# GQA and cross attention joined: the last GQA pair also does the first rows, queries and scores of the cross layer, and the cross layer's pairs run in another order

## The chip, the cores and the metric

The kernel runs on one core of one Trainium2 chip. The metric is the device time of one execution in microseconds (us), the median of the runs. A core has five engines that run side by side, each in its own program order, and meet only at semaphores: TensorE (PE in the profile, PEld its weight loads), VectorE (DVE), ScalarE (ACT), GpSimd (POOL), and SyncE (SP), which issues the DMA transfers here. TensorE's clock has two levels, 1.2 and 2.4 GHz; the profile gives the granted clock as a share of the higher.

## The reference, cut to what matters

Four layers follow one another on `x` (16 rows of 128 positions by 512) with the context `ctx_2048` of the same shape.

```python
x = _L0_xattn_ref(ctx_2048, x, ...)   # latent attention, RMS norm, MLP
x = _L1_xattn_ref(x, ctx_2048, ...)   # grouped attention (GQA): LN(attention(x, ctx) Wo + bo + x) gamma + beta
x = _L2_xattn_ref(x, ctx_2048, ...)   # cross attention, MLP
x = _L3_xattn_ref(ctx_2048, x, ...)   # latent attention, RMS norm, MLP

# _L2_xattn_ref (cross), shortened
x = layer_norm(hidden_states, ln1_w, ln1_b)
q = x @ q_w + q_b
k = encoder_hidden_states @ k_w + k_b
v = encoder_hidden_states @ v_w + v_b
attn = softmax(where(mask, q k^T / sqrt(HD), mask_value))     # 16 heads of 32
hidden = (attn v) @ cproj_w + cproj_b + hidden_states
y = layer_norm(hidden, ln2_w, ln2_b)
return hidden + gelu(y @ fc_w + fc_b) @ proj_w + proj_b
```

Each row depends only on itself: row b of the cross layer needs row b of GQA alone.

## The kernel before, in words

The 16 rows go through a layer in 8 pairs. Each layer has one function per engine (`pe_gqa`, `act_gqa`, `dve_gqa`, `pool_gqa`, `sp_gqa` and the same with `cross`), which lists that engine's work by hand. The order in these lists is the order of execution.

A pair has rounds: four in GQA, two in cross. A round is: scores on PE into four score banks (`pe_scores`; in cross a mask matmul closes each bank), a maximum on DVE (`dve_max`), exponentials on ACT with the row sum (`act_exp`, four segments for each of four banks; in cross they read the score bank and free it, in GQA DVE has copied the scores already), the reciprocal on DVE (`dve_invert`), the multiplication on POOL (`pool_norm`, 16 instructions), the transposes of the probabilities on PE (`pe_turn_probs`, four times four), their copies out of PSUM (two on ACT, `act_probs`; two on DVE, `dve_probs`), and the product with the values (`pe_attend`). Then the heads are taken out with a high and a low part (`act_heads`, `dve_heads`), the output projection runs for each row (`pe_out`), DVE adds the residual and takes the moments (`dve_out`), and POOL normalizes (`pool_root`). In GQA the normalized row is the cross layer's residual; it is normalized once more for the cross layer's queries (`dve_again`, `pool_again`), and SP stores both to HBM.

All products are float32 in three passes over high and low parts (`three_passes`, L324). Inputs of a pair are loaded, turned by PE (`pe_turn_x`), taken out by ACT and DVE (`act_x`, `dve_x`) and projected (`pe_queries`). In cross `act_x` is eight small activations with the layer norm's scale and bias into the buffer `affine` (L780), and `dve_x` makes the high part (L1064) and the low part (L1066) from it. Cross keys and values are computed during GQA, stored to HBM and reloaded per pair.

All PSUM results but the scores go through a ring of four banks (`begin`): each waits until the result four before it has been taken out. `act_round` and `dve_round` interleave one round's maxima or exponentials with the copies of another's transposes, and call `between()`, which holds the `act_x` or `dve_x` of a next pair. In the cross layer before, `between()` is filled in round 1 of a pair, for the next pair.

In a cross pair PE's list is: scores of round 1, transposes of round 0, x transposes of the next pair, output of the odd row of the last pair, attend 0, queries of the next pair (two blocks), scores of round 0 of the next pair, transposes of round 1, output of the even row, attend 1. Between the layers PE does the last GQA output (row 15), the x transposes, queries and first scores of cross pair 0. On DVE the order there is: `dve_again` of row 14, `dve_out` of row 15, `dve_again` of row 15, mask, `dve_x` of cross pair 0, and POOL does the normalizations of rows 14 and 15 between, then two tile splits (`split_tile`) of the cross output weights.

## Time and profile before

| | us |
|---|---|
| timed runs, median (lowest, highest) | 2624.87 (2624.17, 2631.24) |
| the profiled execution | 2633.31 |
| its span in the trace | 2631.4 |
| PE busy | 2473.8 (94%) |
| ACT, POOL, DVE busy | 1088.4, 1114.7, 1224.5 |
| mean granted clock of TensorE | 0.971 |

PE is busy in nearly all of the span. What is not PE time, or is PE time at the lower clock, shows in the slices of the page and in stretches of the trace. The GQA layer lies at about 840 to 1212 us from the span's start, the cross layer's attention at about 1212 to 1482, its MLP behind. All times of stretches and rows below are in us from the span's start.

### The profile page before, as it was taken

Reading aid. Unit: us, or ns where it says so; the run is one execution under the profiler, and the core shown is the slowest. Engines: PE = TensorE matmul, PEld = TensorE weight load, DVE = VectorE, ACT = ScalarE, POOL = GpSimd, SP = SyncE. Lnnn points to the kernel's source line nnn. Section 1 sums busy time; section 2 is a strip of 40 time slices with the busy share of each in tenths; the row PEclk is TensorE's granted clock in tenths of the full one; section 3 lists DMA queues with packets and bytes.
Section 4 is the critical chain, followed back from the end, with each engine's and each line's share of the span. In section 5 each row is a group of like instructions: output and inputs, shape, how many; then the busy total and the mean of one; then the engine's idle time right before and its main releaser. Section 6 shows DMA issues by size and latency. Waiting matters only on the chain.

```text
span 2631.4 us, 48760 instructions
## 1 busy us (share of the span) xinstructions
PE 2473.8 (94%) x18464; PEld 2073.3 (79%) x18464; DVE 1224.5 (47%) x3295; ACT 1088.4 (41%) x3705; POOL 1114.7 (42%) x1972
## 2 busy tenths in 40 slices
PE   7999998999999999986888899999999999899999
PEld 5888886888888888875777788887788888688887
DVE  4555555233224677674555532332355555432322
ACT  4555554111115777774666311111455555311111
POOL 2453445500063778776575740014144443730000
PEclk9999999999999999996898999999999999999999
DMA  4111312211033232223343330122112211320100
GB/s 158 58 57 57 102 53 81 76 48 49 28 95 107 96 122 99 88 82 126 109 142 121 123 97 18 48 68 65 49 50 79 68 41 57 101 66 31 49 32 16
DMA packets 106614, 198.07 MB, mean 75 GB/s; under 512 B 8272, under 2 KB 35600, under 8 KB 103312
## 3 DMA queue, kind: packets, MB, share of 16 engines
q1 hardware_dynamic: 106384, 194.97, 22.4%
q8 instruction: 149, 2.44, 0.4%
q14 instruction: 81, 0.66, 0.1%
HBM read 136.22 MB, written 58.72 MB: 74 GB/s over the span
## 4 chain that ended last, share of the span: by engine, by line
PE 77%; ACT 10%; DVE 7%; POOL 3%; issue 2%; DMA 1%; SPq 0%; DVEq 0%; POOLq 0%; ACTq 0%
PE banks L324 69%; ACT plain_high L715 7%; PE banks L465 4%; PE banks L495 3%; DVE plain_high L970 1%; POOL plain_high L1298 1%; ACT plain_high L699 1%; ACT plain_work L780 1%; DVE stats L1101 1%; PE banks L519 1%; DVE rounded_work L1075 1%; DVE rounded_high L1019 1%; DMA rounded_work<-ctx_split 0%; POOL rounded_high L315 0%; DVE plain_work L1116 0%
## 5 line engine op out<-in xcount | busy, mean ns | idle before, releaser
L324 PE MATMUL banks<-rounded_work,rounded_low 128*128 128x512 f32 (+1 forms) x2688 | 526.0, 350 | 45.2 <-DVE rounded_low L1130 13.7
L1298 POOL TENSOR_SCALAR plain_high<-plain_high,inv_sum 128x128 f32<-128x128 f32 (+1 forms) x1024 | 389.4, 405 | 416.3 <-DVE inv_sum L992 415.9
L324 PEld LDWEIGHTS banks<-rounded_work,rounded_low 128*128 128x128 f32 x2688 | 435.6, 193 | 114.1 <-issue 29.2
L324 PE MATMUL banks<-rounded_work,rounded_high 128*128 128x512 f32 (+1 forms) x2400 | 487.6, 357 | 7.4 <-DMA rounded_work<-ctx_split 7.1
L949 ACT ACTIVATE plain_work<-banks,columns 128x512 f32<-128x512 f32 x192 | 132.5, 690 | 866.9 <-PE banks L324 866.9
L324 PEld LDWEIGHTS banks<-rounded_work,rounded_high 128*128 128x128 f32 x2400 | 398.1, 192 | 75.7 <-DMA rounded_work<-ctx_split 7.7
L1274 DVE CAST rounded_work<-plain_work 128x512 fp32r<-128x512 f32 x192 | 102.1, 532 | 694.0 <-ACT plain_work L949 685.8
L324 PE MATMUL banks<-rounded_low,rounded_work 128*128 128x512 f32 x1728 | 418.2, 394 | 0.0
L324 PE MATMUL banks<-rounded_high,rounded_work 128*128 128x512 f32 (+1 forms) x1728 | 390.2, 377 | 0.0
L324 PEld LDWEIGHTS banks<-rounded_low,rounded_work 128*128 128x128 f32 x1728 | 324.6, 190 | 69.9 <-issue 3.3
L324 PEld LDWEIGHTS banks<-rounded_high,rounded_work 128*128 128x128 f32 x1728 | 309.1, 188 | 60.6 <-issue 1.4
L1442 POOL TENSOR_TENSOR plain_work<-plain_work 128x512 f32<-128x512 f32 x48 | 66.7, 1420 | 613.1 <-DMA plain_work<-x 417.6
L974 DVE TENSOR_REDUCE neg_max<-banks 128x2 f32<-128x512 f32 (+1 forms) x320 | 204.7, 682 | 36.0 <-PE banks L454 36.0
L1298 POOL TENSOR_SCALAR plain_low<-plain_low,inv_sum 128x256 f32<-128x256 f32 x256 | 118.8, 488 | 235.4 <-DVE inv_sum L992 235.4
L715 ACT ACTIVATE plain_high<-banks,neg_max 128x256 f32<-128x256 f32 (+1 forms) x512 | 210.1, 464 | 12.3 <-DVE neg_max L974 12.3
L715 ACT ACTIVATE plain_high<-plain_high,neg_max 128x128 f32<-128x128 f32 x512 | 197.8, 391 | 17.5 <-DVE neg_max L970 17.5
L465 PE MATMUL banks<-ident,plain_high 128*128 128x128 f32 x1280 | 181.1, 297 | 13.4 <-POOL plain_high L1298 9.1
L465 PEld LDWEIGHTS banks<-ident,plain_high 128*128 128x128 f32 x1280 | 154.0, 152 | 33.6 <-issue 18.4
L1276 DVE TENSOR_TENSOR rounded_work<-plain_work,rounded_work 128x512 fp32r<-128x512 f32 x192 | 155.8, 811 | 6.6
L324 PE MATMUL banks<-rounded_work 32*128 32x256 f32 (+1 forms) x3072 | 132.4, 299 | 27.0 <-DVE rounded_work L1046 20.3
L324 PEld LDWEIGHTS banks<-rounded_work 32*128 32x128 f32 x3072 | 109.6, 194 | 60.7 <-issue 55.4
L992 DVE RECIPROCAL inv_sum<-row_sum 128x4 f32<-128x4 f32 (+1 forms) x224 | 41.6, 186 | 211.7 <-ACT plain_high L715 168.7
(101 smaller groups left out, 3069.8 us busy)
## 6 DMA issues: line engine op xcount, KB each, us to landing
plain_work<-x SPq DMA_DIRECT2D x96, 256.0 KB, 3.2
plain_work<-mlp_w SPq DMA_DIRECT2D x96, 256.0 KB, 2.7
rounded_work<-ctx_split SPq DMA_DIRECT2D x16, 1024.0 KB, 6.0
u<-plain_work SPq DMA_DIRECT2D x48, 256.0 KB, 2.6
plain_work<-u SPq DMA_DIRECT2D x12, 1024.0 KB, 7.2
x<-plain_work SPq DMA_DIRECT2D x48, 256.0 KB, 2.2
plain_work<-attention_w SPq DMA_DIRECT2D x44, 256.0 KB, 2.7
plain_work<-inputs_t SPq DMA_DIRECT2D x8, 1024.0 KB, 8.0
```

What stands on the lines that cost most here:

```text
L324: mm = pe.matmul(dst, lhs(i), rhs(j), start=first and n == 0, stop=last and n == 2, skip_group_check=True)
L465: mm = pe.transpose(dst[:, t * P:(t + 1) * P], pr[:, r, t * P:(t + 1) * P], ident[:, :])
L495: mm = pe.matmul(dst[32 * r:32 * r + 32, i * P:(i + 1) * P], v, pt[:, r, at:at + P], start=t == 0, stop=t == n_t - 1, skip_group_check=True)
L519: mm = pe.transpose(dst[:, r * P:(r + 1) * P], u_nat[:, r, f * P:(f + 1) * P], ident[:, :])
L715: last = act.activation(pr[:, r, part], pr[:, r, part] if gqa else PS[:, r, part], ACT.Exp, scale=-1.0 if gqa else 1.0, bias=neg_max[:, R ...
L949: act.activation(gelu[:, j % 2, :], bank(key), ACT.Gelu_apprx_tanh, bias=col(y, 28 + j)).then_inc(evac_of(key), 1)
L974: dve.tensor_reduce(neg_max[:, R % 2, r, 0:y.segs], src.rearrange("p (g n) -> p g n", g=y.segs), AX.X, ALU.max, negate=True).then_inc(maxe ...
L992: dve.reciprocal(inv_sum[:, R % 2, 2 * half:2 * half + 2, 0:y.segs], row_sum[:, R % 2, 2 * half:2 * half + 2, 0:y.segs]).then_inc(inverted, 1)
L1274: dve.tensor_copy(G[:, j % 4, 0, :], gelu[:, j % 2, :]).then_inc(g_hi, 1)
L1276: dve.tensor_tensor(G[:, j % 4, 1, :], gelu[:, j % 2, :], G[:, j % 4, 0, :].bitcast(F32), ALU.subtract).then_inc(g_ready, 1)
L1298: last = pool.tensor_scalar(part, part, inv_sum[:, R % 2, r, g:g + 1], 1.0, ALU.mult, ALU.mult)
L1442: last = pool.tensor_tensor(res[:, r, :], res[:, r, :], wide_bias, ALU.add)
```

## The change

The joint and the cross layer's own order are rewritten on all five engines. Line numbers of the changed kernel differ by a few; the instructions are the same, but for their order and the buffers they use.

In the last GQA pair, where the next pair's inputs and queries would stand, now stand those of cross pair 0, its first scores, and the x transposes of cross pair 1. The GQA output of row 15, its moments and normalizations move into cross pair 0. In the cross pairs the queries of the next pair move up behind the transposes of round 0; attend 0 and the odd row's output stand behind them; the x transposes are those of two pairs ahead and stand behind the transposes of round 1, with `between()` now in the round 0 of the next pair.

```diff
@@ pe_gqa (last pair)
-                if more:
-                    pe_turn_x(pe, y, p + 1)
+                pe_turn_x(pe, *((y, p + 1) if more else (L[2], 0)))
...
-                if more:
-                    pe_queries(pe, y, p + 1, 0)
+                pe_queries(pe, *((y, p + 1) if more else (L[2], 0)), 0)
...
                 if more:
                     pe_values(pe, y, p + 1, 0)
+                else:
+                    pe_queries(pe, L[2], 0, 1)
                 pe_attend(pe, y, p, 2)
                 if more:
                     pe_values(pe, L[2], p + 1, 0)
                     pe_scores(pe, y, p + 1, 0)
+                else:
+                    pe_scores(pe, L[2], 0, 0)
                 pe_turn_probs(pe, y, p, 3)
+                if not more:
+                    pe_turn_x(pe, L[2], 1)
...
-            pe_out(pe, y, B - 1)
@@ pe_cross
-            pe_turn_x(pe, y, 0)
-            for i in range(2):
-                pe_queries(pe, y, 0, i)
-            pe_scores(pe, y, 0, 0)
             for p in range(PAIRS):
                 more = p + 1 < PAIRS
                 pe_scores(pe, y, p, 1)
                 pe_turn_probs(pe, y, p, 0)
-                if more:
-                    pe_turn_x(pe, y, p + 1)
-                if p:
-                    pe_out(pe, y, 2 * p - 1)
-                pe_attend(pe, y, p, 0)
                 if more:
                     for i in range(2):
                         pe_queries(pe, y, p + 1, i)
                 else:
                     for f in range(FB):
                         pe_turn_u(pe, M[y.n], 0, f)
+                pe_attend(pe, y, p, 0)
+                pe_out(pe, *((y, 2 * p - 1) if p else (L[1], B - 1)))
                 if more:
                     pe_scores(pe, y, p + 1, 0)
                 pe_turn_probs(pe, y, p, 1)
+                if p + 2 < PAIRS:
+                    pe_turn_x(pe, y, p + 2)
                 pe_out(pe, y, 2 * p)
                 pe_attend(pe, y, p, 1)
@@ dve_cross
-                dve_round(dve, y, p, 1, (p, 0), inputs)
-                if p:
-                    dve_out(dve, y, 2 * p - 1)
-                dve_heads(dve, y, p, 0)
+                dve_round(dve, y, p, 1, (p, 0), nothing)
...
-                dve_round(dve, y, p + 1, 0 if more else None, (p, 1), nothing)
+                dve_heads(dve, y, p, 0)
+                if p:
+                    dve_out(dve, y, 2 * p - 1)
+                else:
+                    dve_again(dve, L[1], B - 2)
+                    dve_out(dve, L[1], B - 1)
+                dve_round(dve, y, p + 1, 0 if more else None, (p, 1), inputs)
+                if not p:
+                    dve_again(dve, L[1], B - 1)
                 dve_out(dve, y, 2 * p)
                 dve_heads(dve, y, p, 1)
@@ pool_gqa (last pair)
+                if not more:
+                    pool.wait_ge(k_stored, 16 * PAIRS)
+                    pool.wait_ge(v_stored, 16 * PAIRS)
+                    split_tile(pool, ("qo", 2), 4)
+                    split_tile(pool, ("qo", 2), 5)
                 pool_norm(pool, y, p, 3)
                 pool_bias(pool, y, 2 * p + 1)
-                if more:
-                    pool_norm(pool, y, p + 1, 0)
+                if not more:
+                    split_tile(pool, ("qo", 2), 6)
+                pool_norm(pool, *((y, p + 1) if more else (L[2], 0)), 0)
                 pool_root(pool, y, 2 * p)
-            pool_again(pool, y, B - 2)
-            pool_root(pool, y, B - 1)
-            pool_again(pool, y, B - 1)
@@ pool_cross
                 pool_norm(pool, y, p, 1)
+                if not p:
+                    split_tile(pool, ("qo", 2), 7)
+                    pool_again(pool, L[1], B - 2)
+                    pool_root(pool, L[1], B - 1)
                 pool_bias(pool, y, 2 * p)
...
                 if more:
                     pool_norm(pool, y, p + 1, 0)
+                if not p:
+                    pool_again(pool, L[1], B - 1)
                 pool_bias(pool, y, 2 * p + 1)
```

ACT's lists change in the same way as DVE's. SP loads the first cross rows, keys and output weight tiles during the last GQA pair, and the first rows of the MLP (`sp_first_rows`) one pair earlier. So that the first cross round can begin while GQA's probabilities are in use, the cross layer's probabilities and heads move from the slots 12 to 15 to the slots 0 to 3 (`plain_low` and `rounded_low` in the rows below), with the MLP's weight blocks in another order of slots, one buffer of the cross keys moves, and the affine rows of cross pairs 0 and 1 get a buffer of their own (`first_affine`).

PE, at the joint, before. The names: L495 is the attend (`plain_work` in GQA, `plain_high,plain_work` in cross), L324 with `rounded_high` alone an output projection, L359 the x transposes, L324 with 128x256 the queries, L324 with 128x128 and L454 the cross scores with their mask, L465 the transposes of probabilities.

```order
L324 MATMUL banks<-rounded_high 128x512 x12
L495 MATMUL banks<-plain_work 32x128 x16
L324 MATMUL banks<-rounded_high 128x512 x12
L359 MATMUL banks<-ident,plain_work 128x128 x8
L324 MATMUL banks<-rounded_work,rounded_low 128x256 x48
L324 MATMUL banks<-rounded_work 128x128 x48
L454 MATMUL banks<-plain_work,ones_row 128x512 x4
L324 MATMUL banks<-rounded_work 128x128 x48
L454 MATMUL banks<-plain_work,ones_row 128x512 x4
L465 MATMUL banks<-ident,plain_high 128x128 x16
```

The same place on PE after the change, from the attend of GQA's round 2.

```order
L495 MATMUL banks<-plain_work 32x128 x16
L324 MATMUL banks<-rounded_work 128x128 x48
L454 MATMUL banks<-plain_work,ones_row 128x512 x4
L465 MATMUL banks<-ident,plain_high 128x128 x16
L359 MATMUL banks<-ident,plain_work 128x128 x8
L324 MATMUL banks<-rounded_high 128x512 x12
L495 MATMUL banks<-plain_work 32x128 x16
L324 MATMUL banks<-rounded_work 128x128 x48
L454 MATMUL banks<-plain_work,ones_row 128x512 x4
L465 MATMUL banks<-ident,plain_low 128x128 x16
L324 MATMUL banks<-rounded_work,rounded_low 128x256 x48
```

The first cross scores now stand before GQA's last transposes, and the queries of pair 0 stand still further up, one block in each of two GQA rounds.

PE, one cross pair before, from the scores of round 1.

```order
L324 MATMUL banks<-rounded_work 128x128 x48
L454 MATMUL banks<-plain_work,ones_row 128x512 x4
L465 MATMUL banks<-ident,plain_high 128x128 x16
L359 MATMUL banks<-ident,plain_work 128x128 x8
L324 MATMUL banks<-rounded_low,rounded_high 128x512 x12
L495 MATMUL banks<-plain_high,plain_work 32x128 x16
L324 MATMUL banks<-rounded_work,rounded_low 128x256 x48
L324 MATMUL banks<-rounded_work 128x128 x48
L454 MATMUL banks<-plain_work,ones_row 128x512 x4
L465 MATMUL banks<-ident,plain_high 128x128 x16
L324 MATMUL banks<-rounded_low,rounded_high 128x512 x12
L495 MATMUL banks<-plain_high,plain_work 32x128 x16
```

The same pair after the change.

```order
L324 MATMUL banks<-rounded_work 128x128 x48
L454 MATMUL banks<-plain_work,ones_row 128x512 x4
L465 MATMUL banks<-ident,plain_low 128x128 x16
L324 MATMUL banks<-rounded_work,rounded_low 128x256 x48
L495 MATMUL banks<-plain_low,plain_work 32x128 x16
L324 MATMUL banks<-rounded_low 128x512 x12
L324 MATMUL banks<-rounded_work 128x128 x48
L454 MATMUL banks<-plain_work,ones_row 128x512 x4
L465 MATMUL banks<-ident,plain_low 128x128 x16
L359 MATMUL banks<-ident,plain_work 128x128 x8
L324 MATMUL banks<-rounded_low 128x512 x12
L495 MATMUL banks<-plain_low,plain_work 32x128 x16
```

The queries (128x256) moved from directly before the next scores to directly behind the first transposes, and the x transposes (L359) from the first half of the pair to the second.

ACT, one cross pair before, from the copies and exponentials in which round 0 is transposed. L699 is a copy of transposed probabilities, L715 the exponentials, L780 the affines, L729 the heads, L755 the queries.

```order
L699 ACTIVATE plain_high<-banks 128x512
L715 ACTIVATE plain_high,row_sum<-banks,neg_max 128x128 x4
L699 ACTIVATE plain_high<-banks 128x512
L715 ACTIVATE plain_high,row_sum<-banks,neg_max 128x128 x4
L780 ACTIVATE plain_work<-banks,columns 128x128 x8
L715 ACTIVATE plain_high,row_sum<-banks,neg_max 128x128 x8
L729 ACTIVATE rounded_high<-banks,columns 128x128 x4
L755 ACTIVATE rounded_work<-banks,columns 128x256 x4
L699 ACTIVATE plain_high<-banks 128x512
```

ACT after, from the same place.

```order
L697 ACTIVATE plain_low<-banks 128x512
L713 ACTIVATE plain_low,row_sum<-banks,neg_max 128x128 x4
L697 ACTIVATE plain_low<-banks 128x512
L713 ACTIVATE plain_low,row_sum<-banks,neg_max 128x128 x12
L753 ACTIVATE rounded_work<-banks,columns 128x256 x4
L727 ACTIVATE rounded_low<-banks,columns 128x128 x4
L697 ACTIVATE plain_low<-banks 128x512
L713 ACTIVATE plain_low,row_sum<-banks,neg_max 128x128 x4
L697 ACTIVATE plain_low<-banks 128x512
L713 ACTIVATE plain_low,row_sum<-banks,neg_max 128x128 x4
L778 ACTIVATE plain_work<-banks,columns 128x128 x8
L713 ACTIVATE plain_low,row_sum<-banks,neg_max 128x128 x8
```

The affines (L780, now L778) moved from the exponentials of round 1 to those of the next pair's round 0, and the queries stand before the heads.

## Rows read from the trace of the kernel before

**Rows 1.** Stretches: from:to, length, busy PE PEld DVE ACT POOL, granted clock, DMA share, GB/s.
```profile
1168.96:1276.06 107.10, 72.60 (x729) 61.64 (x729) 50.68 (x197) 55.21 (x244) 66.30 (x134) 0.75 0.29 105
1276.06:1453.55 177.49, 151.29 (x1682) 129.81 (x1681) 105.69 (x259) 120.24 (x528) 115.25 (x257) 0.91 0.39 133
1453.55:1482.19 28.64, 20.44 (x150) 15.92 (x149) 19.85 (x43) 14.12 (x49) 21.39 (x37) 0.88 0.29 93
```

**Rows 2.** Timeline of PE at the joint: start, duration, instructions, [idle before <-releaser].
```profile
1209.50 2.99 PE L324 MATMUL banks<-rounded_high 128*128 128x512 f32 x12 [1.53 <-issue]
...
1224.49 8.10 PE L324 MATMUL banks<-rounded_work,rounded_low 128*128 128x256 f32 x48 [11.13 <-issue]
1234.63 1.58 PE L324 MATMUL banks<-rounded_work 32*128 32x128 f32 x48 [2.04 <-DVE rounded_work L1046]
```

**Rows 3.** Timeline of DVE at the joint.
```profile
1220.90 0.69 DVE L1101 BATCH_NORM_STATS2 stats<-plain_work 128x6 f32<-128x512 f32 x1 [4.51 <-POOL plain_work L1333]
...
1222.18 0.42 DVE L1064 CAST rounded_work<-plain_work 128x512 fp32r<-128x512 f32 x1
```

**Rows 4.** Timeline of PE in one cross pair.
```profile
1315.30 6.00 PE L324 MATMUL banks<-rounded_work,rounded_low 128*128 128x256 f32 x48 [1.30 <-DVE rounded_work L1066]
1323.34 1.59 PE L324 MATMUL banks<-rounded_work 32*128 32x128 f32 x48 [2.04 <-DVE rounded_work L1046]
...
1325.25 3.42 PE L465 MATMUL banks<-ident,plain_high 128*128 128x128 f32 x16
1328.43 3.02 PE L324 MATMUL banks<-rounded_low,rounded_high 128*128 128x512 f32 x12
1331.38 1.08 PE L495 MATMUL banks<-plain_high,plain_work 128*32 128x128 f32 x32
...
1334.85 2.22 PE L465 MATMUL banks<-ident,plain_high 128*128 128x128 f32 x16
...
1344.27 1.21 PE L324 MATMUL banks<-rounded_work,rounded_low 128*128 128x256 f32 x8 [1.28 <-DVE rounded_work L1066]
```

**Rows 5.** Chain of waits in the same pair: start, duration, engine and line.
```profile
1321.33 0.85 ACT rounded_work L755 x2
1322.21 0.89 DVE rounded_work L1046 x2
...
1326.40 0.60 ACT plain_high L699
1327.00 1.40 ACT plain_high L715 x8
1328.40 0.49 ACT plain_high L699
...
1340.23 2.81 ACT plain_work L780 x8
...
1343.52 0.70 DVE rounded_work L1066
```

**Rows 6.** Timeline of ACT: the heads right behind GQA's last exponentials.
```profile
1198.50 0.60 ACT L729 ACTIVATE rounded_high<-banks,columns 128x128 fp32r<-128x128 f32 x2
```

**Rows 7.** Groups by form, 1276 to 1453.6: count, busy us, mean ns, idle before.
```profile
L1298 POOL TENSOR_SCALAR plain_high<-plain_high,inv_sum 128x128 f32<-128x128 f32 x194 | 68.4, 379 | 58.2 <-DVE inv_sum L992 58.2
```

**Rows 8.** Stretches in the cross layer, columns as in rows 1.
```profile
1305.92:1309.68 3.76, 3.19 (x28) 2.56 (x24) 3.73 (x12) 2.42 (x10) 3.68 (x8) 1.00 0.30 117
1325.00:1329.00 4.00, 4.00 (x23) 3.66 (x20) 3.03 (x5) 2.60 (x12) 0.94 (x2) 0.59 0.37 135
1352.30:1359.00 6.70, 6.68 (x69) 6.26 (x69) 2.72 (x5) 2.29 (x10) 2.43 (x4) 0.50 0.31 108
```

**Rows 9.** Timeline of PE in the tail of the cross layer.
```profile
1470.23 0.66 PE L465 MATMUL banks<-ident,plain_high 128*128 128x128 f32 x4 [1.58 <-ACT plain_work L800]
...
1477.74 4.61 PE L324 MATMUL banks<-rounded_low,rounded_high 128*128 128x512 f32 x12 [2.42 <-DVE rounded_high L1019]
```

More of the change, by code:

```diff
@@ L938, in act_cross @@
                         act_turn_u(act, M[y.n], 0, f)
-                act_round(act, y, p + 1, 0 if more else None, (p, 1), nothing)
+                act_heads(act, y, p, 0)
+                act_round(act, y, p + 1, 0 if more else None, (p, 1), inputs)
                 act_heads(act, y, p, 1)
@@ L1619, in sp_gqa @@
                     sp_next_hidden(sp, y, 2 * p)
+                if not more:
+                    load_tile(sp, ("qo", 2), 6)
+                if p:
                     sp_store_h(sp, y, 2 * p - 1)
```

142 lines of the change are left out of this document (62 added, 80 removed).

## The prediction

> **What bounds the kernel now.** I read the stretches by engine first [rows 1]. All columns are of the one core; times are us from the span's start. In the 107.1 us from the scores of the last GQA pair to the first full cross pair, PE is busy 72.6 us at a granted clock of 0.75 of full speed. In the six cross pairs behind it PE is busy 151.3 of 177.5 us at 0.91, in the tail of 28.6 us 20.4 us. Everywhere else the page shows PE at nine tenths or more, so only these three stretches, here A, B and C, can give much.
>
> Then the PE timeline of the joint [rows 2]: the last output rows of GQA, 11.13 us of idle time, the queries of cross pair 0, and more idle time around its first scores. The profile calls the 11.13 us "issue"; the DVE rows tell what it is [rows 3]. DVE stood 4.51 us for POOL's normalization (L1333) of row 15 and only then, at 1222.18, could split the turned rows of cross pair 0 that PE needs. That is a chain of orders, not of data: the rows of pair 0 have nothing to do with row 15.
>
> Then a cross pair on PE [rows 4]: 1315.30 to 1344.27 is one pair. Its idle times are 2.04 us before the scores (the query split on DVE), 1.28 to 1.30 us before the queries (the split of the x rows), and small ones. Over six pairs the period is 177.49/6 = 29.6 us [rows 1]. The chain of waits of that pair [rows 5] is mostly ACT: copies, exponentials, the affine of the x rows.
>
> **The change, stretch A.** In the last GQA pair ACT gets cross affines (eight activations, 2.81 us, [rows 5]) where it had no inputs; that delays its later rounds by 2.8 us. The first query block adds 0.85 us on ACT and 0.89 us on DVE [rows 5], about 1 us of it on the path. ACT reached the end of the last GQA exponentials at 1198.50 [rows 6]; now 1198.5 + 2.8 + 1.0 = 1202.3. Behind it come the second query block, 0.85 + 0.89 + 0.25 of hand-over, so the first cross scores start at 1204.3. (Before: 1234.63 [rows 2].) POOL's two tile splits ahead of the last GQA norm end that norm near 1208.3, off this path, since the x transposes behind it are wanted by ACT only at 1210.7.
> From there, at full clock:
> - scores 1.9 ([rows 4], 1323.34 to 1325.25), first transposed block and its hand-over 0.6: 1206.8;
> - ACT, copy 0.60, exponentials 1.40, copy 0.49, exponentials 1.40, affines 2.81 = 6.7 [rows 5]: 1213.5;
> - DVE's split of the last x block 0.1 + 0.44 + 0.70 (the second is [rows 5]) = 1.2, the reciprocal and hand-over 0.4, sixteen POOL multiplies at 68.4/194 us each = 5.65 [rows 7], the last transposes 0.6: 1221.4;
> - queries 6.0, attend 1.0, output rows 2.95 [rows 4]: 1231.3; scores 1.9, first block 0.6: 1233.8;
> - ACT 6.7 + the other two exponentials 2.8 = 9.5, hand-over 0.1, scores 1.8: 1245.2.
> Before, this point (the end of the scores of round 1 of cross pair 1) is 1276.06 [rows 1]. The gain is 30.9 us at full clock. It is not all kept. The present stretch runs at 0.75; the new one still idles on PE (3.6 us ahead of the first scores, 2 to 3 us twice later). A fall there costs PE half of the 4.0 to 6.7 us that one lasts [rows 8], 2 to 3.4 us, and part of it is under POOL's time. I take 4 us for two or three falls (bounds 1 and 8). POOL and SP are late in pair 1: the deferred norm of row 15, its store, and the reload of the buffer put POOL's second bias at about 1254, and the norm of round 1 of pair 1 ends 0.7 us after PE wants it. So A gives 30.9 - 4 - 0.7 = 26 (22 to 29).
> What hides the moved work: the GQA output of row 15 (2.95 us on PE) now stands between pair 1's queries and scores, in time in which PE would wait; its normalization (DVE stood 4.51 us for it, [rows 3]) fits POOL's gaps, which was busy 66.3 of the 107.1 us. If that cover is gone, its 4.5 us come back, once.
>
> **Stretch B.** The new pair order puts the queries right behind the transposes of round 0; attend and an output (4 us) now stand between the queries and the scores, which covers the 2.04 us. The x rows are turned one pair early, so the 1.3 us goes too. What is late next: the affines now sit in round 0 of ACT, between its second and third exponentials, and round 1's scores on PE need the last exponential to free its bank. The loop from scores to scores is, in the same terms as above, 0.6 + 6.7 + 1.2 + 0.4 + 5.65 + 0.6 (the norm path) + queries 6.0 + 1.0 + 2.95 + scores 1.9 = 27.0 us. The other branch, through the freed bank, is 0.6 + 9.5 + 0.1 + 1.9 + 2.0 (transposes) + 6.0 + 1.0 + 2.95 + 1.9 = 25.95, so PE has 1.05 us of slack there. PE's own work is about 22.7 us (6.0 + two scores 3.7 + two transposes 4.0 + x transposes 1.1 + two outputs 5.9 + two attends 2.0): it will stand some 2.8 us before round 1's scores and 1.1 us inside the transposes behind them. The two small waits are thus replaced by one larger one. The pair shown took 28.97 with 1.2 us lost to the clock in one transpose group (the sixteen transposes of 1325.25 took 3.42 us, those of 1334.85 2.22, [rows 4]), so the old period at full clock is 27.8 and the average loss 1.8.
> The new wait will make the clock fall too, I think: both falls of [rows 8] followed idle times of 2.0 and 1.3 us within some 9 us. One fall costs 2 to 3.4 us; 1.05 of it is under POOL's time. I take 1.1 net: 28.1 us, or 1.5 less than 29.6. Six periods: 9 us (bounds 27.0, a gain of 15.6, and 29.6, nothing).
>
> **Stretch C.** The transposes for the MLP move ahead of the attend, and ACT's and DVE's part ahead of the heads. Stepping through with the same durations I get out-to-end 24.7 us from the end of the last scores instead of 28.6 [rows 1, 9], with a new PE wait of 3.2 us before the attend, for the first MLP block's evacuation; less 2 us for the clock: 2 us (0 to 4). The reload of the MLP rows one pair early and the other block order of the MLP move no time: PE is busy without a gap there.
>
> **Sum.** 26 + 9 + 2 = 37 us. The profiled execution has a span of 2631.4 and 2633.31 us; it would become 2594.4 and 2596.3. The three timed runs lie lower, median 2624.87; the same 37 us off that is 2588.
>
> **A page against the rows.** The row first: from 1305.92 to 1309.68 PE does 3.76 us of almost nothing but transposes, with 0.55 us of waiting, and the granted clock stays at 1.00, the 2.4 GHz level [rows 8]. The Trainium skill, TensorE: Matmul & The Clock Gate, Part 4: PE-mode transpose, states that transposes do not count as PE busy in the way matmuls do. By that rule the new order, a wait of 2.8 us, 1.9 us of scores and then transposes with gaps, is what the gate punishes, and the time is that of the last rival below; by the row it is my forecast.
>
> **The rivals.** (1) B's period does not shrink: the larger wait costs a fall of 6.7 us in each pair, [rows 8] at 1352.3, or ACT's chain is longer than I added. For it: ACT is the largest part of the chain. 26 + 0 + 2 = 28: 2597. Chance 0.20. (2) The clock never falls in B and the loop runs at 27.0: 28 + 15.6 + 3 = 46.6: 2578. For it: after the wait of 1.30 us the 48 query matmuls still ran at full speed, 6.00 us, and so they do in all six pairs. Chance 0.17. (3) The join does not join: pair 1's residual rows wait for the deferred row 15 (POOL norm, store, reload of the one buffer), SP's queue holds the x rows and keys behind it, and A gives 10 us less: 2598. Against it: I find 4 us of slack at the bias. Chance 0.08. (4) Slower: the low clock (1.2 GHz) begins at round 1's scores in every pair and lasts through the queries. Then scores 1.9, transposes 2.0 and queries 6.0 double, less the 1.05: 27.0 + 8.85 = 35.9, six times 6.3 more than now, +38, against the 28 of A and C: 2635. It decides from a period of 29.6 + 28/6 = 34.3. Against it: no fall in B lasted more than 7 us, and the transposes of [rows 8]. Chance 0.04.
>
> **How the numbers follow.** Forecast 0.50, rivals 0.20, 0.17, 0.08, 0.04, and 0.01 for the rest. The forecast alone spans 2580 to 2597; with rivals 1 and 2 and most of 3 the range is 2574 to 2604. A measurement of this kernel can tell 0.3%, 7.9 us, from no change. All cases but rival 4 and part of 3 are faster by more: faster 0.94, same 0.02, slower 0.04.
>
> **What would show it.** In the profile after: no PE idle of over 4 us between the last GQA pair and cross pair 1; the end of cross pair 1's second scores near 1249 (1245 at full clock); in the cross pairs a wait of 2 to 3 us before round 1's scores, released by ACT's exponentials, and gaps released by POOL's multiply in the transposes behind; no wait before queries or round 0's scores; a period of 27 to 29 us with one fall of the clock in it. A period over 29.6, or a DVE or POOL wait on the residual rows in pair 1, would prove me wrong.

## The result

The changed kernel takes 2580.59 us (median of 4 runs, 2572.21 to 2583.19) where the kernel before takes 2628.05 on the same chip (2624.17 to 2631.62): a ratio of 0.9827, 95% interval 0.9806 to 0.9848. Two repeats on other chips gave 0.9834 (0.9815 to 0.9852) and 0.9837 (0.9823 to 0.9852). The profiled execution has a span of 2581.3 us where it had 2631.4, so 50.1 us less.

The three stretches of [rows 1] in the profile after, in the same columns: from:to, length, busy PE, PEld, DVE, ACT, POOL, granted clock, DMA share, GB/s. The fourth row is a piece of B with the clock at its lower level, and is discussed further down.

```profile
1167.69:1246.78 79.09, 66.27 (x738) 56.40 (x737) 52.92 (x204) 57.45 (x252) 63.89 (x133) 0.87 0.33 111
1246.78:1407.38 160.60, 146.92 (x1673) 126.84 (x1672) 104.28 (x254) 117.08 (x520) 116.72 (x259) 0.94 0.46 157
1407.38:1433.96 26.58, 20.80 (x150) 17.19 (x149) 16.32 (x42) 14.35 (x49) 19.73 (x33) 0.82 0.32 110
1379.80:1386.30 6.50, 6.49 (x59) 6.06 (x60) 5.39 (x15) 3.12 (x14) 6.22 (x16) 0.50 0.11 47
```

A fell from 107.10 to 79.09 us, B from 177.49 to 160.60, C from 28.64 to 26.58: 28.0 + 16.9 + 2.1 = 47.0 us. The other 3 us lie outside: 1.3 ahead of A and 1.9 behind C. The matmuls are the same; in A the idle time went from 34.5 to 12.8 us, and the granted clock rose from 0.75 to 0.87.

PE at the joint, which answers [rows 2]: start, duration, instructions, [idle before <-releaser].

```profile
1203.08 1.59 PE L324 MATMUL banks<-rounded_work 32*128 32x128 f32 x48 [1.85 <-DVE rounded_work L1044]
...
1208.96 3.01 PE L324 MATMUL banks<-rounded_high 128*128 128x512 f32 x12
...
1220.97 6.70 PE L324 MATMUL banks<-rounded_work,rounded_low 128*128 128x256 f32 x48
...
1228.62 3.06 PE L324 MATMUL banks<-rounded_high 128*128 128x512 f32 x12
```

The first cross scores start at 1203.08, 31.6 us earlier than the 1234.63 of [rows 2], before the last two GQA outputs (1208.96 and 1228.62). The 11.13 us of idle time ahead of the queries of cross pair 0 are gone; from here to the end of A no wait is longer than the 1.85 us shown.

PE in a cross pair, which answers [rows 4]. The rows show the waits ahead of and in one period (from 1300.72, the end of round 1's scores, to the next such end at 1327.81, 27.09 us), and below them the transposes and queries of the period that begins at 1355.00.

```profile
1297.61 0.55 PE L324 MATMUL banks<-rounded_work 32*128 32x128 f32 x3 [1.02 <-ACT plain_low L713]
1299.01 1.33 PE L324 MATMUL banks<-rounded_work 32*128 32x128 f32 x37 [0.85 <-ACT plain_low L713]
...
1300.72 3.63 PE L465 MATMUL banks<-ident,plain_low 128*128 128x128 f32 x16
1304.01 6.21 PE L324 MATMUL banks<-rounded_work,rounded_low 128*128 128x256 f32 x48
1310.14 1.08 PE L495 MATMUL banks<-plain_low,plain_work 128*32 128x128 f32 x32
...
1319.20 3.01 PE L324 MATMUL banks<-rounded_low 128*128 128x512 f32 x12 [0.48 <-ACT plain_low L697]
...
1326.10 1.33 PE L324 MATMUL banks<-rounded_work 32*128 32x128 f32 x37 [0.85 <-ACT plain_low L713]
...
1355.00 1.79 PE L465 MATMUL banks<-ident,plain_low 128*128 128x128 f32 x12
1357.55 0.63 PE L465 MATMUL banks<-ident,plain_low 128*128 128x128 f32 x4 [0.76 <-POOL plain_low L1298]
1357.93 5.99 PE L324 MATMUL banks<-rounded_work,rounded_low 128*128 128x256 f32 x48
1363.85 1.08 PE L495 MATMUL banks<-plain_low,plain_work 128*32 128x128 f32 x32
```

No wait stands before the queries (it was 1.30 us) nor before round 0's scores (it was 2.04). In their place two waits, 1.02 and 0.85 us, stand inside round 1's scores, released by ACT's exponentials. The transposes behind them come in two kinds: at 1300.72 at the low clock and without a gap, 3.29 us until the queries, and at 1355.00 at full clock with a gap that POOL's multiply releases, 2.93 us until the queries.

From these rows a period at full clock throughout can be put together, though no period of this trace is one. The transposes take 2.93 us (1355.00 to 1357.93), the queries 5.92 (1357.93 to 1363.85), and from the attend to the end of round 1's scores it is 17.67 (1310.14 to 1327.81). The sum is 26.52 us. The 17.67 us come out the same in the first four periods.

The chain of waits in such a pair, which answers [rows 5]:

```profile
1289.48 0.60 ACT plain_low L697
1290.08 1.00 ACT plain_low L713 x6
...
1293.37 2.79 ACT plain_work L778 x8
1296.16 2.81 ACT plain_low L713 x16
1298.97 0.04 issue
1299.01 1.33 PE banks L324 x37
```

ACT's affines (2.79 us) now lie on the chain between the exponentials. The tail, which answers [rows 9], has the predicted wait of 3.2 us before the attend and keeps the 2.4 us before its last output:

```profile
1416.07 1.08 PE L495 MATMUL banks<-plain_low,plain_work 128*32 128x128 f32 x32 [3.25 <-ACT plain_work L798]
...
1429.62 4.54 PE L324 MATMUL banks<-rounded_low 128*128 128x512 f32 x12 [2.43 <-DVE rounded_low L1017]
```

### The profile page after: what moved, and what is told of

Its sections match the earlier page's. It is cut to its first block, busy times and chain, and to the rows that moved or that the text cites. A ratio compares the mean times of both kernels' runs of the same rounds, so it can differ in the third digit from the quotient of the medians.

```text
span 2581.3 us, 48757 instructions
## 1 busy us (share of the span) xinstructions
PE 2461.0 (95%) x18464; PEld 2065.3 (80%) x18464; DVE 1227.5 (48%) x3295; ACT 1087.8 (42%) x3705; POOL 1110.2 (43%) x1972
## 3 DMA queue, kind: packets, MB, share of 16 engines
q1 hardware_dynamic: 106384, 194.97, 22.6%
## 4 chain that ended last, share of the span: by engine, by line
PE 81%; ACT 9%; DVE 6%; POOL 2%; DMA 1%; issue 1%; SPq 0%; DVEq 0%; POOLq 0%; ACTq 0%
PE banks L324 71%; PE banks L465 5%; ACT plain_high L713 4%; PE banks L495 3%; ACT plain_low L713 2%; DVE plain_high L968 2%; ACT plain_work L778 1%; DVE stats L1099 1%; PE banks L519 1%; POOL plain_low L1298 1%; DVE rounded_work L1073 1%; DMA rounded_work<-ctx_split 1%; DVE plain_work L977 1%; PE banks L454 0%; ACT plain_work L697 0%
## 5 line engine op out<-in xcount | busy, mean ns | idle before, releaser
L324 PE MATMUL banks<-rounded_work,rounded_low 128*128 128x512 f32 (+1 forms) x2688 | 528.1, 351 | 23.2 <-DVE rounded_low L1128 13.8
L324 PEld LDWEIGHTS banks<-rounded_work,rounded_low 128*128 128x128 f32 x2688 | 438.0, 194 | 90.0 <-issue 18.0
L324 PE MATMUL banks<-rounded_work,rounded_high 128*128 128x512 f32 (+1 forms) x2400 | 485.8, 356 | 9.3 <-DMA rounded_work<-ctx_split 8.9
L324 PEld LDWEIGHTS banks<-rounded_work,rounded_high 128*128 128x128 f32 x2400 | 397.0, 191 | 77.0 <-DMA rounded_work<-ctx_split 9.6
L1298 POOL TENSOR_SCALAR plain_high<-plain_high,inv_sum 128x128 f32<-128x128 f32 (+1 forms) x768 | 296.0, 408 | 335.1 <-DVE inv_sum L990 334.7
L324 PE MATMUL banks<-rounded_low,rounded_work 128*128 128x512 f32 x1728 | 416.3, 392 | 0.0
L324 PE MATMUL banks<-rounded_high,rounded_work 128*128 128x512 f32 (+1 forms) x1728 | 390.2, 377 | 0.0
L324 PEld LDWEIGHTS banks<-rounded_low,rounded_work 128*128 128x128 f32 x1728 | 323.2, 189 | 69.1 <-issue 3.0
L324 PEld LDWEIGHTS banks<-rounded_high,rounded_work 128*128 128x128 f32 x1728 | 309.1, 188 | 60.6 <-issue 1.4
L1298 POOL TENSOR_SCALAR plain_low<-plain_low,inv_sum 128x128 f32<-128x128 f32 (+1 forms) x512 | 209.2, 430 | 272.9 <-DVE inv_sum L990 272.5
L713 ACT ACTIVATE plain_low<-banks,neg_max 128x128 f32<-128x128 f32 (+1 forms) x512 | 210.3, 465 | 5.2 <-DVE neg_max L972 5.1
L324 PEld LDWEIGHTS banks<-rounded_work 32*128 32x128 f32 x3072 | 109.6, 190 | 56.7 <-issue 39.7
L324 PE MATMUL banks<-rounded_work 32*128 32x256 f32 (+1 forms) x3072 | 133.8, 295 | 20.7 <-ACT plain_low L713 13.0
L465 PE MATMUL banks<-ident,plain_high 128*128 128x128 f32 x1024 | 132.8, 282 | 13.9 <-POOL plain_high L1298 13.6
L465 PEld LDWEIGHTS banks<-ident,plain_high 128*128 128x128 f32 x1024 | 112.7, 143 | 26.8 <-issue 15.8
```

What stands on the lines that cost most here:

```text
L324: mm = pe.matmul(dst, lhs(i), rhs(j), start=first and n == 0, stop=last and n == 2, skip_group_check=True)
L465: mm = pe.transpose(dst[:, t * P:(t + 1) * P], pr[:, r, t * P:(t + 1) * P], ident[:, :])
L713: last = act.activation(pr[:, r, part], pr[:, r, part] if gqa else PS[:, r, part], ACT.Exp, scale=-1.0 if gqa else 1.0, bias=neg_max[:, R ...
L1298: last = pool.tensor_scalar(part, part, inv_sum[:, R % 2, r, g:g + 1], 1.0, ALU.mult, ALU.mult)
```

## The experiments

All are compared by stretch (A: from the scores of the last GQA pair's round 1 to the end of cross pair 1's second scores; B: six periods from there; C: the tail), since the part of the program ahead of A, which no experiment touches, itself differs by up to 9 us from one profiled execution to the next (A starts between 1160.40 and 1169.35). "Period" is from one end of round 1's scores to the next.

**The join alone.** The joint as in the changed kernel, but for the x transposes of cross pair 1, which go back into cross pair 0 with the rest of the pair's old order. The core of the edit on PE, against the changed kernel (ACT, DVE follow):

```
@@ pe_cross
+                    pe_turn_x(pe, y, p + 1)
+                pe_out(pe, *((y, 2 * p - 1) if p else (L[1], B - 1)))
+                pe_attend(pe, y, p, 0)
...
-                pe_attend(pe, y, p, 0)
-                pe_out(pe, *((y, 2 * p - 1) if p else (L[1], B - 1)))
...
-                if p + 2 < PAIRS:
-                    pe_turn_x(pe, y, p + 2)
```

> The joint of the change with the old order inside the cross pairs (x transposes of the next pair and affines in round 1, queries before the next scores). The trace after splits the gain of 50 us of span into about 28 us at the joint (A), 17 us in the six cross periods (B) and 2 us in the tail (C). If these parts are independent, this kernel keeps A alone: ratio to the kernel before 0.989 (2596 to 2604 us), and the cross periods are again 29 to 30 us. Rival: the parts feed each other (the early x transposes of pair 1 and the output of row 15 behind attend 0 are what lets the joint close), then A alone gives under 20 us, ratio 0.993 or more.

**The order alone.** The pair's order and the tail as in the changed kernel, the joint as before (queries and first scores of cross pair 0 behind the last GQA output). The core on PE, again against the changed kernel:

```
@@ pe_gqa and pe_cross
+            pe_out(pe, y, B - 1)
...
+            pe_turn_x(pe, y, 0)
+            for i in range(2):
+                pe_queries(pe, y, 0, i)
+            pe_scores(pe, y, 0, 0)
+            pe_turn_x(pe, y, 1)
```

> The old joint with the new order inside the cross pairs and in the tail. If the parts are independent: the periods are 27.1 us and the last one 24.4 us, the tail 26.6 us, together 19 us of gain, ratio 0.9928 (2605 to 2612 us), and the 11 us gap at the joint stays. Rival: the new order gains only because the joint primes it; then under 10 us, ratio over 0.996.

Measured against a kernel before of 2626.11 us: the join alone 2601.50 (ratio 0.9912, 0.9894 to 0.993), the order alone 2602.55 (0.9919, 0.99 to 0.9939). By stretch:

| us | A | B | C |
|---|---|---|---|
| before | 107.10 | 177.49 | 28.64 |
| join alone | 76.34 | 179.65 | 28.85 |
| order alone | 105.04 | 160.78 | 26.57 |
| both | 79.09 | 160.60 | 26.58 |

The two parts are nearly separate: the join is worth A (30.8 us) and nothing in B and C; the order is worth B and C (16.7 and 2.1 us) and 2.1 in A. 24.6 and 23.6 us of the two totals add up to 48.2, and the whole change gave 47.5. The order was thus worth far more in B and C (16.7 + 2.1 us) than the 9 + 2 us that the prediction gave it, and its total came out 2.5 us below the range expected here. The join alone loses 2 us in B because its first period is 34.5 us; the other five take 28.4 to 30.0. In the first, PE waits for the transfer of the x rows and then works at the low clock:

```profile
1250.80 1.94 PE L359 MATMUL banks<-ident,plain_work 128*128 128x128 f32 x8 [2.90 <-DMA plain_work<-x_unit]
```

**Affines in halves.** Does the loop go through ACT's affines? Each activation over 128 columns becomes two over 64:

```
-                    last = act.activation(aff_rows(p, i)[:, f * P:(f + 1) * P], bank(key)[:, f * P:(f + 1) * P], ACT.Identity,
+                    for h in range(2):
+                        part = slice(f * P + 64 * h, f * P + 64 * h + 64)
+                        last = act.activation(aff_rows(p, i)[:, part], bank(key)[:, part], ACT.Identity,
```

> The changed kernel with each of the eight affine activations of a cross pair cut into two of half the width; the same result, about 2.3 us more on ACT for each pair (16 at some 0.32 us against 8 at 0.35). My loop says that ACT's affines lie on the path of every period that has them: five periods 27.1 to 29.4 us, and up to 2.3 us for each of the three pairs at the joint: 12 to 18 us slower than the changed kernel, ratio to before 0.987 to 0.990. Rival (PE or POOL is the bound of the period, ACT has slack): under 4 us slower, ratio 0.984 or less.

2599.52 us, 0.9901 (0.9885 to 0.9918). B rises from 160.60 to 178.11 us. Its five periods with affines take 30.3 to 30.9 us, more than the 29.4 that I expected at most; the last one, which has no affines, stays at 24.6. From the chain of waits and the PE timeline of this kernel:

```profile
1303.23 4.74 ACT plain_work L780 x16
1307.97 2.81 ACT plain_low L713 x16
```
```profile
1309.42 0.90 PE L324 MATMUL banks<-rounded_work 32*128 32x128 f32 x3 [2.94 <-ACT plain_low L713]
1310.82 2.39 PE L324 MATMUL banks<-rounded_work 32*128 32x128 f32 x37 [0.50 <-ACT plain_low L713]
```

The affines are 1.95 us longer (4.74 against 2.79), the period 3.7. The rest is the clock. Behind the longer wait (2.94 us) the scores take 2.39 us instead of 1.33, and all in all they end 1.5 us later for it; the queries take 6.3 to 6.5 us until the attend, where it is 5.9 to 6.2 in the changed kernel. With this the branch through the freed bank is the longer one: the transposes behind have no gap that POOL releases, so POOL's time no longer hides the low clock.

**Affines wide.** The same from the other side: one activation over 512 columns for four over 128.

```
-                for f in range(FB):
-                    last = act.activation(aff_rows(p, i)[:, f * P:(f + 1) * P], bank(key)[:, f * P:(f + 1) * P], ACT.Identity,
-                                          bias=col(y, 24 + f), scale=col(y, 20 + f))
+                last = act.activation(aff_rows(p, i), bank(key), ACT.Identity, bias=col(y, 24), scale=col(y, 20))
```

> The changed kernel with one activation over 512 columns for the affine of an x row where there are four over 128 (two for eight in a pair): the scale and the bias of the first block serve for all four, so the layer norm's own parameters of the other three blocks are left out. Theory (ACT's affines are on the loop): they take 2.8 us there now and would take about 1.0, so the cross periods that have affines go from 27.1 to 25.3 us (the last, without them, stays at 24.4), 5 times 1.8 us, and the joint gives one or two times 1.8: 9 to 12 us in all, 0.35 to 0.45% less than the changed kernel. Rival (PE's own work and the low clock bound the period, the affines only fill a wait): 27.1 us as now, total unchanged. Second rival: the path through POOL takes over at about 26.3, half of the gain.

2568.07 us, 0.9798 (0.9783 to 0.9813), 12.2 less than the changed kernel on the same chip (2580.26). The periods are 27.42, 25.87, 25.51, 25.50, 25.49 and 24.86, and A is 74.52. The affines are 1.4 us shorter (two of 0.68 for 2.79), the period 1.6. The theory holds in both directions: ACT's affines are on the loop. The 1.6 us has two parts, though. From 1266.52 to 1383.93 the granted clock is 1.00, so these periods have no fall of the clock; set against the 26.5 us of a full-clock period, the loop is 1.0 us shorter, and the remaining 0.6 is the clock. That the loop gives 1.0 and not 1.4 shows in the chain of waits: behind the first affine (0.68) stands DVE's split of that row (0.44 + 0.69), which takes longer than the second affine. The chain has turned to DVE and POOL, as the second rival had it, though at 25.5 and not at 26.3:

```profile
1312.00 0.68 ACT plain_work L777
...
1312.70 0.44 DVE rounded_work L1060
...
1313.17 0.69 DVE rounded_work L1062
...
1315.13 5.61 POOL plain_low L1296 x16
...
1321.51 5.74 PE banks L324 x48
```

**Half of the norm.** Is POOL's norm on the loop, and does it hide the low clock? POOL multiplies only two of the four column blocks of each row in the cross layer:

```
-                for g in range(y.segs):
+                for g in range(2 if y.kind == CROSS else y.segs):
```

> The changed kernel with only two of the four column blocks of each row tile normalized by POOL in the third layer: half of the normalizing multiplications of that layer is left out. In the changed kernel the cross pairs with all their parts take 26.8 to 28.0 us (27.09 to 27.19 for three of them), and POOL's sixteen multiplies (5.65 us) are the last thing before the transposes. Theory (the loop of 27.0 us through ACT's affines, DVE's split, POOL's norm): the norm path is 2.8 us shorter, the other branch through the freed bank, 25.95 us, is the bound, and the falls of the clock that lay under POOL's multiplies are now on the path: 26 to 27 us. Rival 1 (a low clock costs nothing there whatever stands beside it): 26.0 us, no spread. Rival 2 (POOL is not on the path): 27.1 us as now, the gaps in the transposes released by something else.

One execution, 2573.95 us, span 2572.1; B 159.12 us with periods 27.18, 26.07, 29.33, 26.95, 26.96, 22.63. The mean of the five with affines is 27.3 us: no gain, although the transposes no longer wait for POOL.

```profile
1291.80 1.56 PE L324 MATMUL banks<-rounded_work 32*128 32x128 f32 x37 [0.85 <-ACT plain_low L713]
...
1294.17 3.67 PE L465 MATMUL banks<-ident,plain_low 128*128 128x128 f32 x16
1297.50 6.92 PE L324 MATMUL banks<-rounded_work,rounded_low 128*128 128x256 f32 x48
```

The longest period, 29.33 us, is the branch through the freed bank (25.95 in the prediction) with everything slow in it: 3.33 us from the transposes' start to the queries instead of 2.0, queries of 6.92 instead of 6.00, the next scores 2.39 instead of 1.33; the sum is 25.95 + 1.3 + 0.9 + 1.1 = 29.3. So rival 1 (a low clock costs nothing whatever stands beside it) falls: in the changed kernel it is cheap because POOL's multiplies cover the same transposes. Rival 2 isn't excluded for the five periods by their length alone, only by the gap that the row of 1357.55 shows and by the last period, which without affines took 22.6 us where it takes 24.4, 24.3 and 23.7 in the changed kernel and its two repeats. It is a single execution, and no more is taken from it.

**Affines out of the round.** If the affines are on the loop between the exponentials, they can go out from between them: PE turns the x rows behind attend 0, ACT does the affines and DVE the splits ahead of round 0.

```
@@ pe_cross, act_cross, dve_cross
+                if p + 2 < PAIRS:
+                    pe_turn_x(pe, y, p + 2)
...
-                act_round(act, y, p + 1, 0 if more else None, (p, 1), inputs)
+                inputs()
+                act_round(act, y, p + 1, 0 if more else None, (p, 1), nothing)
```

> The changed kernel with the x transposes of a cross pair moved from behind the transposes of round 1 to behind attend 0, and the affines and splits from between the exponentials of round 0 to the gap of ACT behind the heads. My loop says: without the 2.8 us of affines the norm path is 0.6 + ACT 3.9 and 2.8 + POOL and so on, about 24.9 us against 27.1, the wait before round 1's scores shrinks to about 1.5 us or less: 10 to 12 us faster than the changed kernel, ratio to before 0.978 to 0.979. Rival (the order is not what bounds the period, or DVE's splits now delay the residual rows and the maxima by as much): within 3 us of the changed kernel, ratio 0.982 to 0.984.

2584.43 us, 0.9847 (0.9829 to 0.9865): no gain over the changed kernel, and B is 167.22 us, 6.6 longer. The rival came true here: ACT's chain was shorter, but DVE's was not. DVE in one pair, and PE at two places:

```profile
1312.11 1.23 DVE L1063 CAST rounded_work<-plain_work 128x512 fp32r<-128x512 f32 x1 [0.27 <-ACT plain_work L778]
1313.37 0.98 DVE L1065 TENSOR_TENSOR rounded_work<-plain_work,rounded_work 128x512 fp32r<-128x512 f32 x1
1314.27 1.50 DVE L1063 CAST rounded_work<-plain_work 128x512 fp32r<-128x512 f32 x1
...
1318.21 1.28 DVE L973 TENSOR_REDUCE neg_max<-banks 128x4 f32<-128x512 f32 x2
```
```profile
1254.81 1.94 PE L359 MATMUL banks<-ident,plain_work 128*128 128x128 f32 x8 [4.56 <-DMA plain_work<-x_unit]
...
1322.13 1.08 PE L495 MATMUL banks<-plain_low,plain_work 128*32 128x128 f32 x32 [1.56 <-DVE plain_low L978]
```

The splits of the x rows now stand ahead of the round's maxima on DVE: the first maximum runs at 1318.21, 3 us after its scores, and round 1's attend, whose last inputs DVE copies between these maxima, waits (1.56 us here). And the x rows, now wanted earlier, come late (4.56 us once, up to 1.8 in the other pairs): SP issues their load behind the stores of the pair.

**Both mended.** DVE splits the x rows between the two reciprocals of round 0; SP loads them ahead of the stores.

```
@@ dve_round
+            if k is not None and late:
+                dve_invert(dve, y, p, k, (0,))
             between()
             if k is not None:
-                dve_invert(dve, y, p, k)
+                dve_invert(dve, y, p, k, (1,) if late else (0, 1))
@@ sp_cross
-                if p:
-                    sp_store_h(sp, y, 2 * p - 2)
-                    sp_store_u(sp, y, 2 * p - 2)
...
+                if p:
+                    sp_store_h(sp, y, 2 * p - 2)
+                    sp_store_u(sp, y, 2 * p - 2)
```

> The kernel with the affines out of the round (the earlier experiment in which ACT has them behind the round's exponentials and PE turns the x rows behind attend) with two mends: DVE splits the x rows between the two reciprocals of round 0 where they stood ahead of the round's maxima, and the load of the next x rows is issued ahead of the stores of the pair. Theory (the earlier one gained nothing since DVE's splits came ahead of the maxima and the x rows' transfer was late): the loop is 0.6 + 3.9 + 1.2 + 0.4 + 5.65 + 0.6 + 10 + 1.9 = 24.3 us instead of 27.1, no wait of PE for the x rows' transfer, and the total is 12 to 14 us under the changed kernel, ratio to the kernel before 0.977 to 0.978. Rival 1 (the order around the affines moves only who waits; PE at its clock of these stretches bounds the pair): 27 to 28 us, ratio 0.983 to 0.985. Rival 2: the x splits, now behind the first reciprocal, hold up the second half's norm and the pair stays at 26, ratio 0.980.

> The changed kernel as it is, on the same chip as the others, so that they can be set against it: 0.981 to 0.985 of the kernel before, the three stretches together within 2 us of 266.3 us.

2576.34 us, 0.9825 (0.9806 to 0.9844), against 2580.26 (0.9834) for the changed kernel beside it, whose stretches were 77.17, 160.97 and 26.52. The total is 3.9 us below the changed kernel and misses my 12 to 14, yet four of the six periods come near the 24.3 that was expected: they are 34.75, 26.06, 24.60, 24.90, 25.08 and 24.34. Most of the loss is the first, and PE and SP show it:

```profile
1256.53 1.94 PE L359 MATMUL banks<-ident,plain_work 128*128 128x128 f32 x8 [4.75 <-DMA plain_work<-x_unit]
1258.12 5.06 PE L324 MATMUL banks<-rounded_low 128*128 128x512 f32 x12
```
```profile
1246.06 0.32 SPq L1499 DMA_DIRECT2D x_unit<-plain_work  x1
...
1248.42 0.91 SPq L1479 DMA_DIRECT2D plain_work<-x_unit  x2
```

The rows of pair 3 are issued at 1248.42, behind the store at 1246.06 which waits for the last GQA row's norm, and PE stands 4.75 us for them, then works at the low clock (5.06 us for an output that takes 3.0).

**Rows early at the joint.** That load goes ahead of the last GQA row's stores:

```
@@ sp_before_cross
             for b in range(2):
+                if b:
+                    wait_filled(sp, ("X", y.n, 2, 1))
+                    sp_x(sp, y, 3)
                 sp_store_h(sp, prev, B - 2 + b)
@@ sp_cross
-                if far and p:
+                if far and p > 1:
```

> The kernel of the run before (affines out of the round, x splits between the reciprocals, x rows loaded ahead of the stores) with one more move: at the joint SP issues the load of cross pair 3's x rows between the hidden rows of pair 0, ahead of the stores of the last GQA row, where they stood behind them and behind pair 2's mask, keys and values and were issued at 1248.42. Theory (the 4.75 us that PE stood for these rows at 1256.53, with the low clock behind it, is all that keeps pair 1 at 34.8 us): the first period becomes 25 to 26.5, stretch B 150 to 152 us instead of 159.7, the total 8 to 10 us less than that kernel, 2565 to 2568, ratio to the kernel before 0.977 to 0.979. Rival: the period stays over 31 us since POOL's norms of the last GQA row and pair 1's own stand next in line; at most 4 us less.

> The changed kernel once more, beside the last one on the same chip: 0.982 to 0.985 of the kernel before.

2566.69 us (4 runs, 2563.74 to 2570.13), 0.9789 (0.9774 to 0.9805); the changed kernel beside it 2579.69 (5 runs, 2576.50 to 2582.26), 0.9837. This version is 13.0 us faster than the changed kernel and 56.0 us faster than the kernel before. The stretches and two parts of a pair:

```profile
1162.96:1237.15 74.19, 62.56 (x737) 52.94 (x737) 52.08 (x199) 57.70 (x252) 62.06 (x124) 0.91 0.36 126
1237.15:1390.51 153.36, 145.11 (x1672) 125.61 (x1673) 105.42 (x258) 116.81 (x520) 125.34 (x267) 0.93 0.47 162
1390.51:1415.19 24.68, 18.42 (x149) 15.21 (x149) 16.39 (x43) 14.32 (x49) 19.02 (x33) 0.93 0.25 81
1289.85:1314.72 24.87, 22.97 (x281) 19.77 (x281) 17.34 (x43) 19.96 (x88) 21.67 (x45) 1.00 0.48 168
1264.67:1268.20 3.53, 3.51 (x18) 3.14 (x17) 3.49 (x11) 2.14 (x10) 3.53 (x9) 0.52 0.83 282
1268.14:1274.00 5.86, 5.86 (x51) 5.79 (x49) 2.44 (x8) 5.42 (x28) 5.41 (x11) 1.00 0.82 318
```

B is 153.36 us where I expected 150 to 152. The first period is 27.52 (I expected 25 to 26.5): at the low clock its transposes take 4.90 us until the queries instead of about 3.2, and the queries 6.92 instead of 6.0. The others take 24.66 to 26.26. In the period from 1289.85 to 1314.72 PE is busy 22.97 of 24.87 us, at full clock throughout.

## Why the prediction was right, and where it wasn't

The time, 2580.59, lies in the range (2574 to 2604), 7.4 us under the forecast of 2588. The gain was missed by more: 37 us were forecast, and 47.5 were measured, since with the fourth run of the kernel before, which came with the result, its median is 3.2 us higher than the 2624.87 that the forecast started from. In the profiled spans, which differ by 50.1, 3 of the 13 us between lie outside the three stretches, and B alone has 8. One reading was too round: outside the three stretches the page does not show PE at nine tenths everywhere. Slices 1, 7 and 35 of the 40 read 7, 8 and 8; they read 6, 8 and 8 after the change, and none of the argument rests on them.

- **Stretch A: the mechanism and nearly the size.** Predicted 26 (22 to 29), measured 28.0; in the two repeats A was 77.17 and 77.21 us, 29.9 less than before. The first cross scores were to start at 1204.3 and did at 1203.08, as much earlier as A itself starts (1.3 us). At full clock the end was to be at 1245.2, or 1243.9 from that start; it was at 1246.78. So the stretch took 2.9 us more than its full-clock sum, and in the repeats about 1, where I had taken 4 for the low clock and 0.7 for late residual rows. How much of the 2.9 is the clock is not shown by an experiment. That last 0.7 was for nothing: POOL's second bias, which I put at 1254, ran at 1252.99, and nothing on PE waited for it. Rival 3 (the join does not join) is out: the join alone gives 30.8 us.
- **Stretch B: the mechanism right, three terms mis-sized.** ACT's affines are on the loop: the experiments on them move the period both ways. But the gain of 16.9 us lies outside the bounds that I gave B (0 to 15.6), and it was the width of the total's range that took it in. First, the loop itself: the full-clock period from the rows above is 26.52 us, not 27.0. The steps from the attend to the end of the scores take 17.67 where my sum has 17.95, and the queries and the transposes take 0.1 less each. Second, "I take 1.1 net: 28.1 us" for the clock. The five periods with affines take 26.79, 27.15, 27.09, 27.19 and 28.01, on average 27.25, so the clock costs 0.7 us each. I had one fall cost 2 to 3.4 us of PE's time; in four of the five periods the scores run at full speed (1.33 us) and the fall meets the transposes, of which POOL's multiplies hide all but 3.29 - 2.93 = 0.36 us, and the head of the queries. Only at 1379.81 did it cover scores and transposes together (the 6.50 us at 0.50 shown above), and the period that ends with these scores is 28.01, 1.5 us over full clock. Third, "Six periods": the last pair has no x rows to turn, so no affines, and took 24.37 us, near 27.0 - 2.8. That the loop of 27.0 lies so near the measured 27.25 is partly luck: it is 0.5 us too long, and the clock adds 0.7. The parts add up: 5 x (28.1 - 27.25) + (28.1 - 24.37) = 4.2 + 3.7 = 8.0 us, which is what B gave beyond the forecast.
- **The waits in B.** Predicted: 2 to 3 us before round 1's scores, released by the exponentials; measured 1.02 + 0.85, and 0.48 ahead of an output. Predicted: a gap of about 1.1 us in the transposes released by POOL; measured 0.76, where the clock is full. None before queries or round 0's scores: so it is.
- **Stretch C.** 2 us predicted, 2.1 measured, and the wait of 3.2 us before the attend is there with 3.25. The 24.7 us that I had stepped through at full clock never showed in the changed kernel (26.58, clock 0.82). In the last experiment C took 24.68 at 0.93, still not at full clock.
- **The rivals.** Rival 1 (B does not shrink, 2597) is out by the table: B shrank 16.9. Rival 2 (the clock never falls, 2578) has the better number, 2.6 us from the result, but not for its reason: the clock does fall, in most periods under cover of POOL. Rival 4 (scores, transposes and queries all slow in every pair) did not come in the changed kernel; the 29.33 of the halved norm is one single such period.
- **The page against the row.** The trace again shows PE at full clock over transposes: in the pair of 24.87 us above, which has 32 of them and 8 of the x rows among its other matmuls, the granted clock is 1.00 throughout. And where the clock was low, at 0.52 from 1264.67 to 1268.20, PE did little but sixteen transposes, and the queries behind them ran at 1.00. The Trainium skill, TensorE: Matmul & The Clock Gate, Part 4: PE-mode transpose, has it that transposes do not count as PE busy in the way matmuls do. These rows speak against that for this kernel, but do not settle it: other matmuls stand close on both sides, and no run here isolates the transposes.

## What to carry to other kernels

When an order is redrawn, write its loop as a sum for each branch, and then ask for each iteration whether it has every term: the first and the last often don't. In these runs the low clock cost little where POOL bounded the same stretch, so price it after the branch is chosen; where the cover goes, as with the halved norm, the price comes back. Before an operation is moved out of a loop on one engine, follow its successor on the next engine and its input on the DMA queue: here both took the gain until they were moved along.

## What the hardware showed that I had not expected

- **An affine activation from PSUM costs mostly its start.** In the chains of waits one takes 4.74/16 = 0.30 us over 64 columns, 2.79/8 = 0.35 over 128 and 0.68 over 512: about 0.24 us for each and 0.05 more for every 64 columns.
- **DVE and POOL slow each other.** The cast of an x row takes 0.43 us in the changed kernel and 1.23 and 1.50 us with the affines out of the round. There POOL ran these at the same time:

```profile
1311.76 1.29 POOL L1308 TENSOR_TENSOR plain_work<-plain_work 128x512 f32<-128x512 f32 x1 [0.56 <-DMA plain_work<-x]
1312.99 0.81 POOL L313 CAST rounded_high<-plain_work 128x512 fp32r<-128x512 f32 x1
1313.88 1.60 POOL L315 TENSOR_TENSOR rounded_high<-plain_work,rounded_high 128x512 fp32r<-128x512 f32 x1
```

The first cast, begun at 1312.11, ends 0.3 us after POOL's first operation, and the second, begun at 1314.27, 0.3 us after its third. POOL pays too: its cast takes 0.81 us where it takes 0.61 in the changed kernel, and in the fastest version, where DVE's splits fall into POOL's sixteen multiplies, these take 6.78 us instead of 5.57:

```profile
1310.56 6.78 POOL L1301 TENSOR_SCALAR plain_low<-plain_low,inv_sum 128x128 f32<-128x128 f32 x16 [2.38 <-DVE inv_sum L991]
```

The Trainium skill, SBUF — State Buffer, section SBUF: two separate sides, states that DVE (in a mode that uses both of its ports, or with two inputs in SBUF against a GpSimd operation that reads SBUF) and GpSimd take one pair of ports as an exclusive lock, and the loser blocks for the whole instruction. These rows agree with it; no run here isolates it. In the fastest version it is 1.2 us of the norm in the pairs with affines, and might be the next thing to move; no run tried it.
